# Ternary feed-forward: gate and up products of one token group beside the transform and down products of the group before it

## What is computed

```python
gate = bitlinear(x, w_gate)                 # 512 -> 2048
up = bitlinear(x, w_up)                     # 512 -> 2048
y = h_bitlinear(silu(gate) * up, w_down)    # 2048 -> 512

def act_quant(x):        # per token, 8 bits
    scale = 128 / clip(max(abs(x)), 1e-5)
    return clip(round(x * scale), -128, 127) / scale
def weight_quant(w):     # -1, 0 or 1, times the mean magnitude
def bitlinear(x, w):     return act_quant(x) @ weight_quant(w).T
def h_bitlinear(x, w):   return act_quant(fwht(x)) @ weight_quant(w).T
```

## Time and profile before

| | |
|---|---|
| median of three runs | 3193.43 us (3192.65, 3193.43, 3210.16) |
| the profiled execution | 3183.28 us, its span 3181.5 us |
| granted TensorE clock, mean over the span | 0.884 |
| busy over the span: TensorE, VectorE, ScalarE, GpSimd | 72%, 73%, 57%, 58% |
| the stage of `ternary_ffn` without its weight preparation | from 1099.8 to 1615.9 us |

### The profile page before, as it was taken

The page is one execution under the profiler, slowest core; times in us unless marked ns, Lnnn a source line. Parts: engine busy times, 40 slices in busy tenths (PEclk is TensorE's granted clock), DMA queues, the critical chain, the costliest instruction groups (busy, mean ns, idle before and its releaser), DMA issues. The chain is left out here.

```text
span 3181.5 us, 41697 instructions
## 1 busy us (share of the span) xinstructions
PE 2294.3 (72%) x11062; PEld 1033.6 (32%) x11062; DVE 2335.6 (73%) x3282; ACT 1829.2 (57%) x3160; POOL 1857.6 (58%) x1599
## 2 busy tenths in 40 slices
PE   2999999999995068667637777777778520799990
PEld 0344444444442023223212323233323220455550
DVE  4888888888885866666548988888988473466666
ACT  1888889888884023233217878787878510344440
POOL 2777777777774020120127878787978546677760
PEclk9999999999998579889868989899999755899995
DMA  4232332333322340000011111111010100666656
GB/s 114 60 70 48 63 63 47 66 63 61 65 40 88 128 168 1 0 0 0 0 41 33 28 29 31 31 28 36 23 36 17 41 17 1 186 193 196 202 164 278
DMA packets 158718, 219.28 MB, mean 69 GB/s; under 512 B 29278, under 2 KB 117982, under 8 KB 155408
## 3 DMA queue, kind: packets, MB, share of 16 engines
q1 hardware_dynamic: 138896, 180.22, 21.7%
q0 software_dynamic: 17408, 33.67, 3.2%
q10 hardware_dynamic: 2304, 4.20, 0.3%
HBM read 125.55 MB, written 58.88 MB: 58 GB/s over the span
## 5 line engine op out<-in xcount | busy, mean ns | idle before, releaser
L354 POOL TENSOR_TENSOR a_p_l<-a_probs,a_p_h 128x512 f16<-128x512 f32 x1024 | 1183.0, 1172 | 397.1 <-ACT a_p_h L565 388.2
L559 ACT ACTIVATE a_probs<-a_ps_st 128x512 f32<-128x512 f32 x1024 | 590.9, 594 | 254.7 <-PE a_ps_st L43 236.2
L632 DVE TENSOR_REDUCE a_negmax<-a_ps_max 128x1 f32<-128x512 f32 x1024 | 670.4, 681 | 57.2 <-PE a_ps_max L432 48.6
L565 ACT ACTIVATE a_p_h<-a_probs 128x512 f16<-128x512 f32 x1024 | 637.7, 628 | 1.3
L466 PE MATMUL a_ps_o<-a_p_h,a_v_h 128*128 128x512 f16 x1024 | 400.3, 391 | 2.5 <-POOL a_p_l L354 1.9
L680 DVE RECIPROCAL a_sums<-a_sums 128x128 f32<-128x128 f32 x384 | 355.8, 936 | 20.1 <-ACT a_plain L577 20.0
L899 POOL TENSOR_TENSOR f_hl<-f_h,f_hh 128x2048 f16<-128x2048 f32 x16 | 65.1, 4068 | 375.3 <-ACT f_hh L1003 375.3
L432 PE MATMUL a_ps_max<-a_k_st,a_q_st 96*128 96x512 f16 x512 | 210.2, 411 | 96.0 <-DVE a_negmax L632 79.5
L43 PE MATMUL a_ps_st<-a_q_st,a_k_st 100*128 100x512 f16 x512 | 207.4, 405 | 21.2 <-ACT a_probs L559 20.9
L432 PE MATMUL a_ps_max<-a_k_hh,a_q_hl 128*128 128x512 f16 x512 | 196.3, 384 | 22.7 <-DMA a_k_lo<-a_qk_l 20.4
L471 PE MATMUL a_ps_o<-a_p_l,a_v_l 128*128 128x512 f16 x512 | 205.2, 401 | 0.0
(11 more groups left out here) (297 smaller groups left out, 4722.9 us busy)
## 6 DMA issues: line engine op xcount, KB each, us to landing
s_raw<-in_guT SPq DMA_DIRECT2D x32, 768.0 KB
a_k_hh<-a_qk_h SPq DMA_DIRECT2D x64, 256.0 KB, 5.1
m_y_tok<-f_nothing SPq DMA_DIRECT2D x16, 1024.0 KB, 12.9
c_yg<-m_y_tok SPq DMA_DIRECT2D x16, 1024.0 KB, 8.2
a_ctx_in<-in_ctx SPq DMA_DIRECT2D x32, 256.0 KB, 2.6
a_q_hl<-a_qk_h SPq DMA_DIRECT2D x32, 256.0 KB, 4.4
a_q_hm<-a_qk_h SPq DMA_DIRECT2D x32, 256.0 KB, 5.0
a_q_hl<-a_qk_l SPq DMA_DIRECT2D x32, 256.0 KB, 5.0
```

Of the source, the lines that this page charges most:

```text
L354: pool.tensor_tensor(p_l[:, h % 2, j, :], probs[:, h % RAWS, j, :], p_h[:, h % 2, j, :], ALU.subtract).then_inc(p_split, 1)
L559: act.activation(probs[:, h % RAWS, j, :], ps_st[:, j % 2, :], ACT.Exp, scale=1.0 if L0 else DH1 ** -0.5).then_inc(exped, 1)
L565: act.activation(p_h[:, h % 2, j, :], probs[:, h % RAWS, j, :], ACT.Copy).then_inc(p_high, 1)
L632: dve.tensor_reduce(negmax[:, h % 2, t:t + 1], ps_max[:, t % 2, :], AX.X, ALU.max, negate=True).then_inc(maxed, 1)
```

## The change

The two phases of a group become one pipeline over 83 slots, and everything is written out without a loop. Slot `n` up to 63 makes the gate and up products of chunk `n` (16 per group, four groups). From slot 19 on (`LAG`), four slots in a row also carry one tile of the transform and down work: slots 0 and 1 of the four hold the transform, one bank in front of the up product and one behind it, slot 2 the down products of the tile before, slot 3 the transposes. Tile `i` starts in slot `19 + 4i`, so the last 19 slots have no gate and up products.

With it go these edits:

- PSUM is shared out anew: `ps_f` (four banks) for the transform, one bank each for gate and up (`ps_gu`), one for the quantised transposes (half a tile at a time, `ps_qT`), one for down products, token transposes and token scales (`ps_misc`). In slots 0 to 15 the gate and up products also use `ps_f`, in turns of three.
- The butterflies go to GpSimd, except for the blocks of four chunks 0, 2 and 3. They write to `hb`, and `h`, `h2`, `hb` have one buffer each. `hh`, `hl`, `xqT`, `gscale` have two.
- The magnitude is taken bank by bank (`peak_of`), and ScalarE rounds inside PSUM, in halves; VectorE clips from PSUM, in halves.
- Normalising and rounding the tokens moves to ScalarE (`normalise`, `quantise_tokens`); VectorE measures (`measure_tokens`) and clips while it copies the transposed tokens out of PSUM (`keep_tokens`).
- The silu is made in place. The clearing transfers read a source of 128 columns, so that each moves runs of 512 bytes where it moved 2048.

The core of the diff:

```diff
+    CH = (B // G) * NC_
+    LAG = 19
...
+    VECTOR_BLOCKS = (0, 2, 3)
...
+        h, h2, hb = (sb(n, [P, NB, G * P], F32) for n in ("h", "h2", "hb"))
+        hh, hl = sb("hh", [P, 2, NC_, G * P], F16), sb("hl", [P, 2, NC_, G * P], F16)
...
-        STEPS = 1 + 2 * NA + 5 * G + PREP
+        nothing = sb("nothing", [P, P], F32)
+        ps_f = ctx.enter_context(nc.psum_tensor("f_f", [P, NB, NA * P], F32))
+        ps_gu = ctx.enter_context(nc.psum_tensor("f_gu", [P, 2, G * P], F32))
+        ps_qT = ctx.enter_context(nc.psum_tensor("f_ps_qT", [P, NC_ // 2, P], BF16))
+        ps_misc = ctx.enter_context(nc.psum_tensor("f_misc", [P, D], F32))
...
+            if n < NC_ and n % 3:
+                return ps_f[:, 2 * (n % 3) - 2, :], ps_f[:, 2 * (n % 3) - 1, :]
+            return ps_gu[:, 0, :], ps_gu[:, 1, :]
...
+            return n - 3 if n < NC_ else n - 1
...
+            return ((n - LAG) // 4, (n - LAG) % 4) if n >= LAG else (None, None)
...
+        HIGH_AT = {NB * A + (6 if A in VECTOR_BLOCKS else 7 if A == 1 else 5): A for A in range(CH // NB)}
...
+                sp.dma_start(lower.rearrange("(p k) (c n) -> p (k c) n", k=SEL, n=P), nothing[:, :].unsqueeze(1).to_broadcast([P, SEL * KD, P])).then_inc(lower_cleared, 16)
...
+            if step == 0:
+                eng.wait_ge(h_ready, NB * A + NB)
+                need(eng, butterflied, 2 * A)
+                eng.tensor_tensor(h2v[:, :, 0, :], hv[:, :, 0, :], hv[:, :, 1, :], ALU.add).then_inc(paired, 1)
+            elif step == 1:
+                eng.tensor_tensor(h2v[:, :, 1, :], hv[:, :, 0, :], hv[:, :, 1, :], ALU.subtract).then_inc(paired, 1)
+            elif step == 2:
+                eng.wait_ge(paired, 2 * A + 2)
+                need(eng, low_done, A)
+                eng.tensor_tensor(hb[:, 0:2, :], h2[:, 0:2, :], h2[:, 2:4, :], ALU.add).then_inc(butterflied, 1)
+            else:
+                eng.tensor_tensor(hb[:, 2:4, :], h2[:, 0:2, :], h2[:, 2:4, :], ALU.subtract).then_inc(butterflied, 1)
...
+            for A in range(CH // NB):
+                if A not in VECTOR_BLOCKS:
+                    for step in range(4):
+                        butterflies(pool, A, step)
+                g, blk = A // NA, slice(NB * (A % NA), NB * (A % NA) + NB)
+                pool.wait_ge(high_done, A + 1)
+                pool.tensor_tensor(hl[:, g % 2, blk, :], hb[:, :, :], hh[:, g % 2, blk, :], ALU.subtract).then_inc(low_done, 1)
...
+                need(pe, gate_scaled, same_banks_before(n) + 1)
+                block_products(nc, banks(n)[0], [(wg[:, k, cols], xqT[:, g % 2, k, :]) for k in range(KD)], True, True).then_inc(g_done, 1)
...
+                need(pe, h_ready, same_banks_before(n) + 1)
+                block_products(nc, banks(n)[1], [(wu[:, k, cols], xqT[:, g % 2, k, :]) for k in range(KD)], True, True).then_inc(u_done, 1)
...
+                if bb == 0:
+                    pe.wait_ge(low_done, NA * g + NA)
+                if bb % 2 == 0:
+                    need(pe, q_ready, 2 * (i - 1) + bb // 2 + 1)
+                if i == 0:
+                    pe.wait_ge(h_ready, NC_)
+                block_products(nc, ps_f[:, bb, :], [(x[:, g % 2, NB * a + bb, tokens(t)], had[:, a, :]) for a in range(NA) for x in (hh, hl)],
+                               True, True).then_inc(f_done, 1)
...
+                pe.wait_ge(q_ready, 2 * i + half + 1)
+                need(pe, qT_kept, 2 * i + half)
...
+                pe.wait_ge(qT_kept, 2 * i + half + 1)
+                if half == 0:
+                    need(pe, y_added, i)
+                    pe.wait_ge(xT_kept, tiles)
+                    pe.wait_ge(gs_ready, spreads)
...
+            for n in SLOTS:
+                i, s = tile_slot(n)
+                if n < CH:
+                    gate_product(n)
+                if s in (0, 1):
+                    transform(i, 2 * s)
+                elif s == 2 and i > 0:
+                    down(i - 1, 0, tiles_before(n), spreads_before(n))
+                elif s == 3:
+                    transpose_quantised(i, 0)
+                if n < CH:
+                    up_product(n)
+                if s in (0, 1):
+                    transform(i, 2 * s + 1)
+                elif s == 2 and i > 0:
+                    down(i - 1, 1, tiles_before(n), spreads_before(n))
+                if next_tile(n) is not None:
+                    transpose_tokens(next_tile(n), downs_before(n))
+                if n % NC_ == NC_ - 1 and n + 1 < CH:
+                    spread_scales(n // NC_ + 1, downs_before(n))
+                if s == 3:
+                    transpose_quantised(i, 1)
+            for half in range(2):
+                down(B - 1, half, B, B // G)
...
+            def high(A):
+                g, blk = A // NA, slice(NB * (A % NA), NB * (A % NA) + NB)
+                act.wait_ge(butterflied, 2 * A + 2)
+                need(act, f_done, NC_ * (g - 1))
+                act.activation(hh[:, g % 2, blk, :], hb[:, :, :], ACT.Copy).then_inc(high_done, 1)
...
+            def round_half(i, half):
+                if half == 0:
+                    act.wait_ge(scale_ready, i + 1)
+                f = ps_f[:, 2 * half:2 * half + 2, :]
+                act.activation(f, f, ACT.Identity, bias=magic[:, 0:1], scale=small[:, i % 2, 4:5]).then_inc(rounded, 1)
...
+            def keep_half(i, half):
+                act.wait_ge(q_tposed, 2 * i + half + 1)
+                need(act, y_done, i)
+                act.activation(qT[:, NC_ // 2 * half:NC_ // 2 * half + NC_ // 2, :], ps_qT[:, :, :], ACT.Copy).then_inc(qT_kept, 1)
...
+            for n in SLOTS:
+                i, s = tile_slot(n)
+                if s == 0 and i > 0:
+                    keep_half(i - 1, 1)
+                if s == 2:
+                    round_half(i, 0)
+                    round_half(i, 1)
+                if s == 3:
+                    keep_half(i, 0)
+                if tile_entering(n, 3) is not None:
+                    normalise(tile_entering(n, 3))
+                if n < CH:
+                    silu(n)
+                if n in HIGH_AT:
+                    high(HIGH_AT[n])
+                if tile_entering(n, 2) is not None:
+                    quantise_tokens(tile_entering(n, 2))
+            keep_half(B - 1, 1)
...
+            def combine_up(n):
+                dve.wait_ge(silued, n + 1)
+                dve.wait_ge(u_done, n + 1)
+                if n % NB == 0:
+                    need(dve, paired, n // NB * 2)
+                if n == 0:
+                    dve.wait_ge(had_set, 1)
+                dve.scalar_tensor_tensor(h[:, n % NB, :], gate[:, n % 2, :], HS, banks(n)[1], ALU.mult, ALU.mult).then_inc(h_ready, 1)
...
+            def peak_of(i, bb):
+                dve.wait_ge(f_done, NB * i + bb + 1)
+                dve.tensor_reduce(peak[:, i % 2, bb:bb + 1], ps_f[:, bb, :], AX.X, ALU.max, apply_absolute_value=True).then_inc(peaked, 1)
...
+            def scale_tile(i):
+                sm = lambda c: small[:, i % 2, c:c + 1]
+                peak_link(dve.tensor_scalar(sm(0), amax[:, i, 0:1], means[:, 1:2], FF ** -0.5 / (128.0 * HS), ALU.mult, ALU.mult))
+                dve.wait_ge(peaked, NB * i + NB)
+                peak_link(dve.tensor_reduce(sm(1), peak[:, i % 2, :], AX.X, ALU.max))
+                peak_link(dve.tensor_scalar(sm(2), sm(1), sm(0), Q_EPS, ALU.mult, ALU.max))
+                peak_link(dve.reciprocal(sm(3), sm(2)))
+                dve.tensor_scalar(sm(4), sm(3), sm(0), 128.0, ALU.mult, ALU.mult).then_inc(scale_ready, 1)
+                peak_link(dve.tensor_scalar(sm(5), sm(2), means[:, 2:3], 1.0 / 128.0, ALU.mult, ALU.mult))
...
+            def quantise_half(i, half):
+                dve.wait_ge(rounded, 2 * i + half + 1)
+                need(dve, q_tposed, 2 * (i - 1) + half + 1)
+                dve.tensor_scalar(q[:, HALF * half:HALF * half + HALF], ps_f[:, 2 * half:2 * half + 2, :].rearrange("p a n -> p (a n)"), -MAGIC, 127.0,
+                                  ALU.add, ALU.min).then_inc(q_ready, 1)
...
+            def add_tile(i):
+                dve.wait_ge(y_done, i + 1)
+                xb = x_all[:, i, :]
+                dve.scalar_tensor_tensor(xb, ps_misc[:, :], small[:, i % 2, 5:6], xb, ALU.mult, ALU.add).then_inc(y_added, 1)
+                dve.wait_ge(y_added, i + 1)
+                dve.bn_stats(stats[:, i, :], xb)
...
+            for n in SLOTS:
+                i, s = tile_slot(n)
+                if n < CH and n > 0 and next_tile(n - 1) is not None:
+                    keep_tokens(next_tile(n - 1))
+                if n < CH and n > 0 and n % NC_ == 0:
+                    keep_scales(n // NC_)
+                if n == LAG:
+                    combine_up(n - 1)
+                if s == 1:
+                    peak_of(i, 1)
+                if s == 2:
+                    peak_of(i, 3)
+                    scale_tile(i)
+                if s == 3 and i > 0:
+                    add_tile(i - 1)
```

(57 more changed lines are left out.)

329 lines of the change are left out of this document (117 added, 212 removed).

## The result

The changed kernel took **3063.11 us** in the median of four runs (3056.81 to 3071.20), the kernel before 3193.04 in the same series (3185.08 to 3210.16). The ratio is 0.9593, its 95% interval 0.9564 to 0.9621: faster by 4.1%. The forecast was 3061. A later series gave 3051.79 against 3186.57, so an agreement within 2 us says little. The profiled execution took 3071.20 us, its span is 3069.1, its mean granted clock 0.898 where it was 0.884.

A forecast was written before the change was run, and what follows sets the result against it. Engines took turns, none full; with turns filled, TensorE's work should bind. 70 + 234 + 59 = 363 us against 492, and 5 from the start, rounded to 132 less: 3051, plus a 10 us gap, 3061 us; range 3035 to 3115.

The forecast's parts named there:

- Overlap: Ternary stage: gate/up and transform/down phases run beside each other, TensorE's own work becomes the bound; 363 us against 492.
- The tile in the steady part: Twelve tiles beside gate products: 19.2 us each with scales, plus 1.2 us for `hl` at three group starts; 234 us.
- GpSimd's sum: Butterfly of 1024 float32 elements on GpSimd: taken at 2.04 us, half of `hl`; range 1.22 to 4.07.
- Filling: Slots 0 to 18, first gate product to first transform: 68.3 us plus 2 for TensorE's slow start, 70 us.
- Emptying: Last four tiles, without chunks beside them: 6.9 + 3 x 13.3 and 12 behind the last transform, 59 us.
- Start: From landing of the constants to first gate product: 12.6 us instead of 17.7, 5 us less.
- Clearing transfers: Transfers with runs a quarter as long: would end near 1310 at worst, before the stage's end near 1480; no cost.
- Rival 1: Steady part: one-element VectorE operations wait for GpSimd, 2 to 4 us per tile; 3085 to 3109 us, chance 0.13.
- Rival 2: Steady part: GpSimd is the bound at 4.07 us per butterfly, 24 us per tile; 3129 us, chance 0.05.
- Rival 3: Steady part: short stalls keep TensorE's clock at 1.2 GHz, 37 us per tile; 3277 us, chance 0.03.
- Rival 4: Each tile: a misplaced wait puts the phases in turn again, 24 to 28 us; 3120 to 3165 us, chance 0.06.
- Rival 5: Better than forecast: collisions while the pipeline fills are milder (15 us of them); 3040 us, chance 0.07.

## Why the prediction was right, step by step

- **Overlap.** It is the cause: undone, the gain is gone. It does not stand alone, though: some 61 us are the overlap with the butterflies where they were, and 47 more come from their move, which pays only with it. The prediction priced both together and did not part them. The stage lost 135.7 us (516.0 to 380.3), 134 were worked out. The medians differ by 129.9 in the first series and by 134.8 in the later one (3186.57 less 3051.79).
- **How close, and how much of it is luck.** The mechanism and the size came as worked out. That 3061 met 3063.11 within 2 us is in part luck: one other layer alone scatters by more than that, and the terms missed in both directions. From the first gate product on, 361 us were measured for 363: the filling took 5 us less than its 70, the twelve tiles 1 more, the emptying 2 more. The start took 1 more.
- **The tile in the steady part.** 19.0, or 19.2 with the scales, and 1.2 for `hl` at each group's start were worked out; 19.01 and 21.16 were measured, and 1185.23 to 1419.98 is 234.8 us for a forecast of 234. The 1.0 us for the scales (eight products) falls whole on the tile at the group's start, with the wait of 1.09 for `hl`. The sum is closer than its parts. Tile 0 takes 21.18 us: TensorE starts it at half clock and has the full clock only from 1190.9 on. The forecast had these 2 us in the filling. The last of the twelve takes 19.14, though only one of its four slots has gate products: TensorE stands 3.1 us for ScalarE's copy and 2.1 for `hl` in it. VectorE's and ScalarE's lists were put too high, at 15.3 and 11.0 us per tile for 13.2 and 9.6 in the mean; neither is the longest. Half of the transform left out shows that TensorE's list is what counts, and that it is only some 1.5 us longer than the round through GpSimd.
- **TensorE's clock as a gain.** The prediction priced the new order at full clock and asked of the clock only whether it would fall. That it would rise is in its sum, but not named: TensorE is busy 36 us less for the same matmuls. In the kernel with the two phases in turn the stage's mean clock is 0.84, with the overlap and GpSimd's butterflies 0.94. No run parts the clock from the waits.
- **GpSimd's sum: mis-sized, hidden.** Taken at 2.04 us from half an `hl`; it takes 2.35, so its block is 13.5 us busy, not 12.2. The range's ends, 1.22 and 4.07, held it. The Trainium skill, "GPSIMD Engine Reference", section "Performance versus the Vector engine", gives GpSimd 1.96 times VectorE's time for a float32 sum; the trace has 2.35 to 1.22, 1.93 times. Taken from there the term would have been right, and nearer to the next bound.
- **Filling.** 68.3 worked out up to the first transform, 65.0 measured. The 2 us for a slow start came too, but behind that transform (0.61 us, and the 21.18 above). Of the 3.3 us, 2.0 are there already at the first block's `hl` (24.4 us after the first gate product for 26.4). VectorE's wait of 4.9 us for `h` and its sum of 5.1 us beside GpSimd's `hl` both came, at their places. Taking block 1 off GpSimd removes both, puts four sums more on VectorE instead, and saves no more than 0.2 to 0.5 us.
- **Emptying.** 59 worked out, 61.2 measured: tiles at 13.66 instead of 13.3, and the first one waits 2.12 us for the last `hl` and starts at half clock.
- **Start.** 12.6 worked out from the landing of the constants (1106.67), 13.6 measured. The activation with a scale and a bias per partition takes 0.80 us on 512 elements; 0.6 had been taken from the silu's 0.62.
- **Clearing transfers.** Nothing was charged, and nothing was seen lost. They are over by about 1164 us, far before the bound of 1310: with runs of a quarter of the length 283 GB/s were moved against about 400 before (from 1110 to 1135 us), not a quarter.
- **Rival 1** is out: the one-element `tensor_scalar` took 0.214 us beside GpSimd's sums, as in the earlier trace rows. VectorE and GpSimd do get in each other's way for SBUF tensors: 5.09 and 1.37 us. **Rival 2**: GpSimd waits 34.9 us for `h` and 38.1 for `hh` in the steady part; it is second, not first. **Rival 3**: the clock was 1.00 from 1190.9 to 1413.7, with stalls of 0.2 to 1.1 us between groups of products and PSUM banks in turns:

```profile
1190.90:1413.70 222.80, 213.45 (x1132) 101.03 (x1129) 155.29 (x289) 111.12 (x128) 156.57 (x59) 1.00 0.00 1
```

The Trainium skill's warning on depth-cycling ("TensorE: Matmul & The Clock Gate", section "A second HAM failure mode: psum-queue depth-cycling") does not show here. **Rival 4**: no wait put the phases in turn. **Rival 5**: the filling came out 3 us shorter, and the emptying took 2 of it back.

## What to carry to other kernels

When no engine is full but they take turns, add up each engine's list for one round of the merged pipeline, at durations from the trace, and walk the chain through once: the longest list plus the stalls on the chain gave the time of a tile inside a group almost to the tenth of a us. Then look for the second longest: here it lies some 1.5 us below the first, so of 3.5 us less work on TensorE only 1.5 came through. A step may go to an engine at which it takes twice as long, if that engine has room in the round and the one it leaves is on the chain; with the overlap gone the same move costs 49 us. What stays unhidden is the filling and the emptying, 65 and 61 of 380 us, and each has its own bound.

## What the runs showed of the hardware

- A sum of 1024 float32 elements per partition: 2.35 us on GpSimd, 1.22 on VectorE; 2048 elements into float16 on GpSimd: 4.08.
- Two operations that both read and write whole SBUF tensors on VectorE and GpSimd took turns: VectorE's sum took 5.09 us where it came second, and GpSimd's 2.58 instead of 2.35 where it did. VectorE's operations with a PSUM input (0.69 and 1.22 us), those of one element (0.15 to 0.21) and its reductions of 512 elements from SBUF (`f_amax`, the statistics: 0.69) kept their times beside GpSimd.
- The second attention layer took 873 and 891 us in two executions of the kernel before and 902 and 912 in two of the changed one, on code that is the same in all four. The ternary stage differed by far less: 516.0 and 517.3 us before, 380.3 and 380.0 after.
